# Second attention: the row maximum and the mask are written into PSUM by ScalarE, three matmul rounds follow, in a new order

## Chip, core and metric

The kernel runs on one core of one Trainium2 chip. The metric is the device time of one execution in microseconds (us). Most executions agree within 0.3%.

## What is computed

The network has four parts one after the other, each added to a residual `x` of 8 batches of 512 rows of 256 numbers (fp32): a first attention, a layer with 16 routed experts, a second attention and a layer with 8 routed experts. The change touches the second attention alone:

```
q = (layernorm(x) @ Wq) * 64 ** -0.5                    # 16 heads of 64
kv = concatenate([layernorm(ctx), layernorm(x)])        # 512 + 512 keys
k, v = kv @ Wk, kv @ Wv
sim = q @ k.T ; sim = sim - max(sim, over keys)
sim = where(mask, sim, -inf)                            # the mask concerns the first 512 keys
x = x + softmax(sim) @ v @ Wo
```

## The kernel before

`layer1_pairs` works in 64 steps: 8 batches times 8 pairs of heads. In step g the softmax and the output of pair g are computed while K, Q, the maxima (and in odd steps V for two pairs) of pair g + 1 are prepared. Head h of a pair lies on partitions 64h to 64h + 63, so two 64-row matmuls, one for each head, run at once; I call such two a round.

The units of a step, as the lists in `WHOLE` name them (one list for even steps, one for odd), and who works on each:

- KK and Q project K and Q of the next pair (L1796), three products each since every operand is split into a high and a low part (fp32r). ScalarE copies the high part (KH L1909, QH L1915), VectorE subtracts for the low part (KL L1956, QL L1961).
- VV0, VV1 project V (L1836, only in odd steps); ScalarE copies (L1921).
- S0 to S7 are rough scores with queries on the partitions (high parts only, L1848), for the row maximum; VectorE reduces them, S0 to S3 with the mask (L1976, two instructions for a tile), S4 to S7 without (L1981). N takes the minimum of the two halves' negated maxima (L1986).
- M brings the negated maxima from columns to rows: four matmuls against an identity (L1858); ScalarE copies into QM (L1925).
- ST0 to ST7 are the exact scores with keys on the partitions, 128 keys by 512 queries by two heads (L1871): four rounds, QM with KM (KM holds a row of ones and a row with the mask, brought by DMAs, L1735), QH with KL, QL with KH, QH with KH. ScalarE takes exp (L1936), GpSimd adds the eight exps up (L2032).
- PV0 to PV7 multiply by V into pO (fp32, L1805); O is ScalarE's copy of it (L1941). den sums the added exps over the keys of the previous step (fp32, L1882), ScalarE copies (L1929); r0 to r3 are reciprocals, after the last one VectorE also multiplies osb by them (L1992, L1996). YY is the product with Wo of the previous step (fp32, L1890), which VectorE adds to the residual (L2001).

Every engine goes through the same list of its parity in that order and does its own share of each unit, so the list is the order of every queue. Tiles of PSUM: pO and pm take one bank each, three slots of two banks serve the units named in `SLOTTED`, dealt in the order of the list, modulo 3 (`slot_of`). `slot_free` makes TensorE wait until the slot's last user has been read. M, Q and den share pm (`BANK`, `use`, `bank`). SyncE's list of DMAs loads weights every second step, K and V inputs once per batch, and the mask rows every step.

## Time and profile before

| | us |
|---|---|
| median of 3 runs | 3544.19 |
| lowest, highest | 3543.92, 3546.04 |
| profiled execution, its own time | 3545.06 |
| its span | 3543.5 |
| the second attention's steps, in the span | about 1054 to 2860 |

A row of the timeline has the start, the duration, the engine, the line, the operation with output and inputs, the count of merged instructions, and in brackets the idle time of the engine before it with what ended it. A matmul's duration is longer than the distance to the next, as they are pipelined.

### The profile page before, as it was taken

To read this page: it belongs to the slowest core of one execution; us is meant where nothing else is said; L and a number is where in the kernel's file an instruction comes from. 1 tells how busy PE (TensorE), PEld (TensorE's weight loads), DVE (VectorE), ACT (ScalarE), POOL (GpSimd) and SP (SyncE) were. 2 spreads that over 40 slices of the span, in tenths; PEclk is the share of its full clock that TensorE was granted. 3 is DMA by queue.
4 is the path that set the end of the run, shared out by engine and by line. 5 is a ranking of instruction groups with operands and counts; after the bars stand their busy time and mean duration, and the time that the engine had idled before them with its cause. 6 is when DMAs were issued, how large, how long until landed. Compare 5 with 4: busy or idle time off the path is not lost. (4 is left out here: it accounts for less than half of the span.)

```text
span 3543.5 us, 56159 instructions
## 1 busy us (share of the span) xinstructions
PE 3194.0 (90%) x17981; PEld 2294.0 (65%) x17982; DVE 2048.6 (58%) x4478; ACT 1267.7 (36%) x1778; POOL 1609.9 (45%) x929
## 2 busy tenths in 40 slices
PE   5875999999439999999999999999999966699988
PEld 4655888888425666666666666666666655577766
DVE  5656555555555666666766667666676653122235
ACT  2332333333234444444444444444444432122222
POOL 4002333333304665666656666556665635500037
PEclk7995999999769999999999999999999958899999
DMA  4000000000471010110101101011010031321223
GB/s 109 1 1 9 14 13 9 13 12 6 151 266 47 31 69 30 65 45 30 68 28 67 45 30 68 27 68 45 30 68 28 7 106 59 133 77 62 63 70 109
DMA packets 89978, 192.94 MB, mean 54 GB/s; under 512 B 12768, under 2 KB 58152, under 8 KB 83760
## 3 DMA queue, kind: packets, MB, share of 16 engines
q1 hardware_dynamic: 73856, 152.84, 12.5%
q0 software_dynamic: 11392, 27.36, 2.5%
q10 hardware_dynamic: 4656, 11.80, 1.0%
q8 instruction: 40, 0.66, 0.1%
q14 instruction: 34, 0.28, 0.0%
HBM read 137.60 MB, written 54.30 MB: 54 GB/s over the span
## 5 line engine op out<-in xcount | busy, mean ns | idle before, releaser
L2032 POOL TENSOR_TENSOR d_acc<-d_acc,d_pr 128x1024 f32<-128x1024 f32 x384 | 938.4, 2444 | 90.9 <-ACT d_pr L1936 60.5
L1936 ACT ACTIVATE d_pr<-d_p 128x1024 f32<-128x1024 f32 x512 | 487.4, 1026 | 235.8 <-PE d_p L1871 235.4
L1805 PE MATMUL d_pO<-d_pr,d_V 128*64 128x512 f32 x2048 | 473.0, 599 | 0.0
L2032 POOL TENSOR_TENSOR d_acc<-d_pr 128x1024 f32<-128x1024 f32 x64 | 153.5, 2399 | 619.8 <-ACT d_pr L1936 619.8
L1981 DVE TENSOR_REDUCE d_nm<-d_p 128x2 f32<-128x1024 f32 x256 | 304.5, 1221 | 95.1 <-PE d_p L1848 95.1
L1976 DVE CUSTOM_DVE_ANT_0 d_biased<-d_p,d_masked 128x512 f32<-128x512 f32 x512 | 330.6, 688 | 32.0 <-issue 32.0
L909 POOL TENSOR_TENSOR e_hs<-e_hf,e_hs 128x512 fp32r<-128x512 f32 x136 | 175.7, 1292 | 365.2 <-ACT e_hs L886 365.2
L1805 PEld LDWEIGHTS d_pO<-d_pr,d_V 128*64 128x64 f32 x2048 | 135.4, 136 | 261.4 <-issue 235.0
L939 DVE SCALAR_TENSOR_TENSOR res<-e_pY,m_Wt,res 128x256 f32<-128x256 f32 x544 | 225.7, 477 | 45.7 <-PE e_pY L847 44.9
L1992 DVE RECIPROCAL d_rb<-d_rb 128x128 f32<-128x128 f32 x256 | 224.6, 919 | 8.6 <-ACT d_rb L1929 8.6
L847 PEld LDWEIGHTS e_pY<-e_Wd,e_hs 128*128 128x128 f32 x1632 | 213.5, 191 | 13.7 <-POOL e_hs L909 2.2
L847 PE MATMUL e_pY<-e_Wd,e_hs 128*128 128x256 f32 x1632 | 217.2, 283 | 2.6 <-POOL e_hs L909 2.6
L930 DVE TENSOR_TENSOR e_hf<-e_sl,e_pU 128x512 f32<-128x512 f32 x136 | 93.7, 689 | 216.1 <-ACT e_sl L883 216.1
L831 PE MATMUL e_pG<-m_XH,e_Wgu 128*128 128x512 f32 x816 | 212.2, 395 | 4.2 <-issue 4.2
L1848 PE MATMUL d_p<-d_KH,d_QH 64*128 64x512 f32 x1024 | 208.4, 443 | 5.2 <-DVE d_nm L1976 2.5
L1848 PEld LDWEIGHTS d_p<-d_KH,d_QH 64*128 64x128 f32 x1024 | 89.0, 184 | 190.2 <-issue 127.9
L1871 PE MATMUL d_p<-d_QM,d_KM 64*128 64x512 f32 x1024 | 208.7, 402 | 0.0
L831 PE MATMUL e_pU<-m_XH,e_Wgu 128*128 128x512 f32 x816 | 208.3, 391 | 0.0
L1921 ACT COPY d_V<-d_p 128x1024 f32<-128x1024 f32 x64 | 64.8, 1012 | 400.2 <-PE d_p L1836 400.2
L1871 PE MATMUL d_p<-d_QH,d_KL 64*128 64x512 f32 x1024 | 202.3, 390 | 0.0
L1871 PE MATMUL d_p<-d_QL,d_KH 64*128 64x512 f32 x1024 | 201.8, 389 | 0.0
L1871 PE MATMUL d_p<-d_QH,d_KH 64*128 64x512 f32 x1024 | 201.7, 388 | 0.0
(288 smaller groups left out, 5621.8 us busy)
## 6 DMA issues: line engine op xcount, KB each, us to landing
d_W<-w_split SPq DMA_DIRECT2D x32, 1536.0 KB, 6.4
kv_split<-c_ys SPq DMA_DIRECT2D x16, 1024.0 KB, 6.4
d_kv<-kv_split SPq DMA_DIRECT2D x8, 2048.0 KB, 10.6
d_masked<-mask_bias SPq DMA_DIRECT2D x64, 256.0 KB
x_slots<-m_zeros SPq DMA_DIRECT2D x1, 9088.0 KB, 29.8
b_x<-x_slots SPq DMA_DIRECT2D x71, 128.0 KB, 2.0
y_slots<-b_y SPq DMA_DIRECT2D x71, 128.0 KB, 1.7
w_split<-c_wq POOLq DMA_DIRECT2D x4, 1536.0 KB, 8.3
```

Of the source, the lines that this page charges most:

```text
L831: last = pe.matmul(out[u % 2][0:fw, :], lhsT, XH[:, xp, k, n * S:(n + 1) * S], start=start, stop=(k == DC - 1 and (wp, xp) == PASSES[-1]))
L847: last = pe.matmul(pY[n % 2][:, t, :], hs[0:fw, u % 2, hp, t * P:(t + 1) * P], Wd[j][0:fw, wp, f, :], start=(f == 0 and m == 0 and t % 2 = ...
L909: pool.tensor_tensor(hs[0:fw, u % 2, LO, :], hf[0:fw, u % 2, :], hs[0:fw, u % 2, HI, :].bitcast(F32), ALU.subtract).then_inc(lo_done, 1)
L939: dve.scalar_tensor_tensor(res[:, tile, :], pY[n % 2][:, t, :], Wt[:, tile, bass.ds(e + column, 1)], res[:, tile, :], ALU.mult, ALU.add).t ...
L1805: last = pe.matmul(pO[own[h], :], V[vb][:, s, par * P + h * HD1:par * P + (h + 1) * HD1], pr[:, s % PT, h, :], start=(s == 0), stop=(s == ...
L1848: last = pe.matmul(out[:, h, :], QH[j][own[h], qt * P:(qt + 1) * P], KH[j][own[h], m * S:(m + 1) * S], start=True, stop=True)
L1871: last = pe.matmul(out[:, h, :], k_[own[h], s * P:(s + 1) * P], q_[own[h], :], start=(i == 0), stop=(i == len(terms) - 1))
L1936: act.activation(pr[:, n % PT, :, :], slot(st, what, n)[:, :, :], ACT.Exp).then_inc(exp_done, 1)
L1976: dve.tensor_tensor_reduce(biased[:, h, :], out[:, h, :], masked[j][:, :], -1.0, MASKED, ALU.add, ALU.min, nm2[:, j, h * TPB + qt, m:m + 1 ...
L1981: dve.tensor_reduce(both, out[:, :, :], AX.X, ALU.max, negate=True).then_inc(max_done, 1)
L1992: dve.reciprocal(rb[:, quarter], rb[:, quarter]).then_inc(r_done, 1)
L2032: pool.tensor_tensor(acc[:, q, :, :], a, pr[:, s % PT, :, :], ALU.add).then_inc(acc_done, 1)
```

## The change

In the transposed scores the round QM with KM goes. In its place the slot is filled before the matmuls: a new unit P0 to P7 on ScalarE writes, for the first four key tiles, the negated maximum plus the mask (`activation` Identity from `nmb`, with a bias column `mcol` for the mask), for the last four the negated maximum alone (`copy`). The three rounds left then accumulate upon it. M now makes the negated maximum in every partition for both heads: eight matmuls whose weights are a column of `nm` repeated (stride 0), into a slot instead of pm, and ScalarE copies 1024 columns to `nmb`. The slot of tile n is taken by P n; ScalarE waits until it is free. The mask comes as one column per key tile, by one DMA of 512 four-byte pieces; KM, its rows and the DMAs for them go. N writes eight numbers per partition side by side. The lists have a new order with P in it, and `start` is set once per bank in VV and YY.

```diff
 WHOLE = (
-    """M KK Q ST0 ST1 ST2 S0 S1 PV0 PV1 S2 ST3 S3 den PV2 PV3 S4 ST4 r0 ST5 r1 r2 ST6 ST7 S5 PV4 r3 PV5 PV6 PV7 O
-       S6 S7 YY N""".split(),
-    """Q KK M VV0 den S0 ST0 ST1 S1 ST2 ST3 ST4 ST5 ST6 r0 ST7 r1 r2 S2 r3 PV0 PV1 PV2 PV3 S3 S4 S5 PV4 PV5 PV6 PV7
-       S6 S7 VV1 N O YY""".split())
-BANK = ("M", "Q", "den")
+    """M Q P0 P1 KK ST0 ST1 S0 P2 den S1 ST2 S2 PV0 PV1 S3 P3 P4 ST3 ST4 S4 S5 P5 PV2 PV3 P6 PV4 P7 ST5 r0 r1 ST6 r2
+       ST7 r3 S6 PV5 PV6 PV7 S7 N O YY""".split(),
+    """Q M P0 VV0 ST0 P1 P2 KK ST1 ST2 den S0 P3 PV0 P4 PV1 ST3 r0 S1 ST4 PV2 S2 PV3 P5 P6 r1 ST5 S3 ST6 P7 PV4 PV5 r2
+       S4 ST7 S5 PV6 r3 PV7 S6 S7 VV1 N YY O""".split())
+BANK = ("Q", "den")
 SLOTS = 3
-SLOTTED = ("ST", "S", "KK", "VV", "YY")
+SLOTTED = ("P", "M", "S", "KK", "VV", "YY")
...
-        QM = sb("d_QM", [P, S], F32R)
+        nmb = sb("d_nmb", [P, 2, S])
+        mcol = [sb(f"d_mcol{j}", [P, TPB]) for j in range(2)]
...
-                            sp.wait_ge(st_done, NKT * st.g)
-                        for h in range(2):
-                            sp.dma_start(KM[j][h * HD1 + 1:h * HD1 + 2, :].bitcast(F32),
-                                         mb[bass.ds(bb, 1), :]).then_inc(mask_in[j], 16)
+                            sp.wait_ge(filled, NKT * st.g)
+                        sp.dma_start(mcol[j][:, :], mb[bass.ds(bb, 1), 0:S].rearrange("o (t p) -> p (o t)", p=P),
+                                     allow_slow_non_contiguous=True).then_inc(mask_in[j], 16)
...
-                            if k_ == "ST":
+                            if k_ == "P":
                                 pe.wait_ge(exp_done, NKT * s.g + m + 1)
+                            elif k_ == "M":
+                                pe.wait_ge(m_read, s.g + 1)
...
-            bank(what)
             pe.wait_ge(max_done, MAXES * st.g + MAXES)
-            for qt in range(TPB):
-                last = pe.matmul(pm[:, qt * P:(qt + 1) * P], nm[:, q, qt, :], identr[:, :], start=True,
-                                 stop=True)
-            last.then_inc(bank_done, 1)
+            out = slot_free(what)
+            for h in range(2):
+                for qt in range(TPB):
+                    last = pe.matmul(out[:, h, qt * P:(qt + 1) * P],
+                                     nm[:, q, h, qt:qt + 1].to_broadcast([P, P]), identr[:, :],
+                                     start=(qt == 0), stop=True, skip_group_check=True)
+            last.then_inc(m_done, 1)
...
                             if s == 0:
-                                pe.wait_ge(bank_read, use(st, "M"))
-                                pe.wait_ge(mask_in[q], 48 * st.by2 + 48)
                                 pe.wait_ge(k_lo, st.g + 1)
-                            out = slot_free(what, n)
-                            terms = [(KM[q], QM), (KL[q], QH[q]), (KH[q], QL[q]), (KH[q], QH[q])]
+                                pe.wait_ge(bank_read, use(step_before(st), "Q"))
+                            pe.wait_ge(filled, T + s + 1)
+                            out = slot(st, "P", n)
+                            terms = [(KL[q], QH[q]), (KH[q], QL[q]), (KH[q], QH[q])]
                             for i, (k_, q_) in enumerate(terms):
                                 for h in range(2):
                                     last = pe.matmul(out[:, h, :], k_[own[h], s * P:(s + 1) * P],
-                                                     q_[own[h], :], start=(i == 0), stop=(i == len(terms) - 1))
+                                                     q_[own[h], :], start=False, stop=(i == len(terms) - 1),
+                                                     skip_group_check=True)
...
-                            act.copy(QM[:, :], pm[:, :]).then_inc(bank_read, 1)
+                            act.wait_ge(m_done, st.g + 1)
+                            if not (isinstance(st.g, int) and st.g == 0):
+                                act.wait_ge(filled, NKT * st.g)
+                            act.copy(nmb[:, :, :], slot(st, what)[:, :, :]).then_inc(m_read, 1)
+                        elif what == "P":
+                            if n == 0:
+                                act.wait_ge(mask_in[q], 32 * st.by2 + 32)
+                                act.wait_ge(m_read, st.g + 1)
+                            for s, (k_, m) in slot_before(st, ("P", n)):
...
+                            if n < TPB:
+                                act.activation(slot(st, what, n)[:, :, :], nmb[:, :, :], ACT.Identity,
+                                               bias=mcol[q][:, n:n + 1]).then_inc(filled, 1)
+                            else:
+                                act.copy(slot(st, what, n)[:, :, :], nmb[:, :, :]).then_inc(filled, 1)
```

## Rows read from the trace of the kernel before

**Rows 1.** Page, section 2: busy tenths and granted clock (tenths) in 40 slices

```profile
PE   5875999999439999999999999999999966699988
...
PEclk7995999999769999999999999999999958899999
```

**Rows 2.** Steady loop: length; busy of PE, PEld, DVE, ACT, POOL; clock; DMA

```profile
1130.40:2795.00 1664.60, 1663.11 (x10212) 1065.24 (x10211) 1132.64 (x2222) 712.96 (x840) 1025.43 (x421) 1.00 0.13 46
```

**Rows 3.** Timeline of ScalarE, one pair of steps

```profile
2019.00 1.01 ACT L1921 COPY d_V<-d_p 128x1024 f32<-128x1024 f32 x1 [10.90 <-PE d_p L1836]
...
2026.51 2.86 ACT L1936 ACTIVATE d_pr<-d_p 128x1024 f32<-128x1024 f32 x3 [0.62 <-PE d_p L1871]
...
2074.44 1.01 ACT L1921 COPY d_V<-d_p 128x1024 f32<-128x1024 f32 x1 [10.88 <-PE d_p L1836]
```

**Rows 4.** Timeline of TensorE, even step

```profile
2020.92 2.98 PE L1796 MATMUL d_p<-d_kv,d_W 128*128 128x512 f32 x12
2023.74 1.52 PE L1796 MATMUL d_pm<-d_kv,d_W 128*128 128x512 f32 x6
2025.19 0.50 PE L1871 MATMUL d_p<-d_QM,d_KM 64*128 64x512 f32 x2
...
2025.99 0.40 PE L1871 MATMUL d_p<-d_QH,d_KH 64*128 64x512 f32 x2
...
2030.80 0.50 PE L1848 MATMUL d_p<-d_KH,d_QH 64*128 64x512 f32 x2
2031.13 0.39 PE L1871 MATMUL d_p<-d_QM,d_KM 64*128 64x512 f32 x2
```

**Rows 5.** Timeline of TensorE, odd step

```profile
2045.30 1.72 PE L1796 MATMUL d_pm<-d_kv,d_W 128*128 128x512 f32 x6
2046.86 2.89 PE L1796 MATMUL d_p<-d_kv,d_W 128*128 128x512 f32 x12
2049.59 0.56 PE L1858 MATMUL d_pm<-d_identr,d_nm 128*128 128x128 f32 x4
2049.99 3.08 PE L1836 MATMUL d_p<-d_W,d_kv 128*128 128x256 f32 x24
2053.00 1.08 PE L1882 MATMUL d_pm<-d_acc,d_ones 128*64 128x512 f32 x4
...
2062.54 3.65 PE L1805 MATMUL d_pO<-d_pr,d_V 128*64 128x512 f32 x16
2066.13 0.96 PE L1848 MATMUL d_p<-d_KH,d_QH 64*128 64x512 f32 x6
```

**Rows 6.** Timeline of TensorE's weight loads, even step

```profile
2028.50 0.19 PEld L1848 LDWEIGHTS d_p<-d_KH,d_QH 64*128 64x128 f32 x2 [0.48 <-ACT d_pr L1936]
```

**Rows 7.** Groups of ScalarE by form: busy, mean ns, idle before

```profile
L1915 ACT ACTIVATE d_QH<-d_pm 128x512 fp32r<-128x512 f32 x64 | 38.3, 599 | 128.1 <-PE d_pm L1796 128.1
...
L484 ACT ACTIVATE a_QT<-a_pQ,a_bqs 128x512 f32<-128x512 f32 x16 | 10.1, 684 | 18.8 <-PE a_pQ L318 18.8
...
L590 ACT COPY m_rows<-m_xh 128x1024 f32<-128x1024 f32 x4 | 4.2, 1040 | 2.0 <-PE m_px L614 2.0
```

**Rows 8.** Page, section 5: groups, busy and mean ns

```profile
L2032 POOL TENSOR_TENSOR d_acc<-d_acc,d_pr 128x1024 f32<-128x1024 f32 x384 | 938.4, 2444 | 90.9 <-ACT d_pr L1936 60.5
...
L1981 DVE TENSOR_REDUCE d_nm<-d_p 128x2 f32<-128x1024 f32 x256 | 304.5, 1221 | 95.1 <-PE d_p L1848 95.1
```

**Rows 9.** N: its line (min/median/max ns); timelines of VectorE and GpSimd

```profile
L1986 DVE TENSOR_TENSOR d_nm<-d_nm x64: 173/1359/1849, 1076.1 to 2823.1; 128x8 fp32r<-128x8 f32 x64
...
2018.09 1.82 DVE L1986 TENSOR_TENSOR d_nm<-d_nm 128x8 fp32r<-128x8 f32 x1
...
2004.66 15.23 POOL L2032 TENSOR_TENSOR d_acc<-d_acc,d_pr 128x1024 f32<-128x1024 f32 x6
```

**Rows 10.** Timeline of TensorE, end of the function

```profile
2827.50 0.63 PE L1871 MATMUL d_p<-d_QH,d_KL 64*128 64x512 f32 x2
2827.93 0.63 PE L1871 MATMUL d_p<-d_QL,d_KH 64*128 64x512 f32 x2
```

More of the change, by code:

```diff
@@ L1619, in use @@
     elif isinstance(st.g, int) and st.g == NSTEP:
-        before = 3 * NSTEP - 1
+        before = 2 * NSTEP - 1
     else:
-        before = 3 * st.g
+        before = 2 * st.g
     return before + bank_uses(st).index(kind) + 1
@@ L1689, in layer1_pairs @@
         MAXES = 3 * TPB + 1
-        SET_UP = 8
+        SET_UP = 2
         def maxes_before(n):
@@ L1713, in _ @@
                 sp.wait_ge(set_up, SET_UP)
-                for j in range(2):
-                    for h in range(2):
-                        sp.dma_start(KM[j][h * HD1:h * HD1 + 1, :].bitcast(F32), onerow[:, :].bitcast(F32)
-                                     ).then_inc(set_rows, 16)
-                sp.wait_ge(set_rows, 4 * 16)
                 sp.dma_start(W[1][:, :, :, :, :].bitcast(F32), wsp[1]).then_inc(w_in[1], 16)
@@ L1923, in emit @@
                         elif what == "M":
-                            act.wait_ge(bank_done, use(st, what))
-                            act.copy(QM[:, :], pm[:, :]).then_inc(bank_read, 1)
+                            act.wait_ge(m_done, st.g + 1)
[7 more added lines that the diff above has]
+                            for s, (k_, m) in slot_before(st, ("P", n)):
+                                if k_ == "P":
+                                    act.wait_ge(exp_done, NKT * s.g + m + 1)
+                                elif k_ == "M":
+                                    act.wait_ge(m_read, s.g + 1)
+                                elif k_ == "S":
+                                    act.wait_ge(max_done, MAXES * pair(s)[1] + maxes_before(m + 1))
+                                elif k_ == "KK":
+                                    act.wait_ge(k_lo, pair(s)[1] + 1)
+                                elif k_ == "VV":
+                                    act.wait_ge(v_read, values_before(s) + m + 1)
+                                else:
+                                    act.wait_ge(y_added, s.g + 1)
+                            if n < TPB:
+                                act.activation(slot(st, what, n)[:, :, :], nmb[:, :, :], ACT.Identity,
+                                               bias=mcol[q][:, n:n + 1]).then_inc(filled, 1)
+                            else:
+                                act.copy(slot(st, what, n)[:, :, :], nmb[:, :, :]).then_inc(filled, 1)
                         elif what == "den":
@@ L1935, in emit @@
                             act.wait_ge(acc_done, 7 * st.g + max(n, 1))
-                            act.activation(pr[:, n % PT, :, :], slot(st, what, n)[:, :, :], ACT.Exp
+                            act.activation(pr[:, n % PT, :, :], slot(st, "P", n)[:, :, :], ACT.Exp
                                            ).then_inc(exp_done, 1)
```

31 lines of the change are left out of this document (11 added, 20 removed).

## The prediction, made before the changed kernel was run

> **What bounds the kernel now.** I read the page first, to see which engine fills the span: in the slices that belong to this function (13 to 32) TensorE shows 9 tenths in every one, at full granted clock [rows 1]. The table by stretches says the same for the steady loop: in 1664.6 us TensorE is busy 1663.1, VectorE 1132.6, ScalarE 713.0, GpSimd 1025.4, the granted clock 1.00, which is the 2.4 GHz level [rows 2]. So the order written for TensorE is nearly free of waits, and what the change is worth is read from TensorE's issue times, not from busy shares (a matmul's bar overlaps the next one's).
>
> I then took the timeline of one pair of steps. The loop's two steps repeat: ScalarE's copy of V at 2019.00 [rows 3] has its twin at 2074.44, 55.44 us later. In the even step, projection of K takes 2.82 us and of Q 1.45; a round of two 64-row matmuls inside the transposed scores takes 0.23 (2025.19 to 2025.99 is 3 rounds and a 0.1 start) [rows 4]. In the odd step Q takes 1.56, M's four matmuls 0.40, VV0 3.01, den and what leads into the next unit 1.0, and four PV units 3.59 [rows 5]. A lone S between fp32 and fp32r work costs 0.33 [rows 4]; of the 3.59, the rounds themselves are 8 times 0.43, so one run of fp32 matmuls costs some 0.15 by itself and 0.10 on the S before it: 0.25 us per switch there and back. I call that the switch price.
>
> **What the change takes from TensorE.** Eight tiles per step lose one round of four: 16 rounds a pair at 0.23 make 3.7 us. M goes from 4 to 8 matmuls of the same shape: plus 0.4 a step, 0.8 a pair (if the stride-0 weights don't overlap with the matmuls, each could take twice 0.1 and M costs 1.6 more in a pair; if the copy is as cheap as now, nothing else; I take 0.1 each, as the row has the same 128x128 form). The new order has more runs of fp32 work: even step, den, PV0-1, PV2-4, PV5-7, YY, five where there were four; odd step seven (den, PV0-1, PV2, PV3, PV4-5, PV6-7, YY) where there were four. Four more at 0.25 are 1.0. The waits of today go: 0.48 before S1 in the even step [rows 6] and some 0.2 in the odd one, 0.7. Without any new wait the pair would be 55.4 - 3.7 + 0.8 + 1.0 - 0.7 = 52.8, 2.6 less. The loop has 31 full pairs: minus 80 us.
>
> **What it adds to ScalarE.** Eight fills of 128x1024 a step. No row shows ScalarE writing PSUM. The nearest is an SBUF to SBUF copy of that size, 1040 ns; a bias pointer costs 684 - 599 = 85 ns on 512 elements [rows 7], so the four masked fills are 1.11 and the four plain ones 1.02 to 1.04; following each other they overlap by 0.10 (three exps take 2.86 in all, one 1.02) [rows 3]. QM's copy of 512 becomes a copy of 1024: 0.59 to 1.01. That is 8.9 us a step on an engine that is busy 713.0 / 30 = 23.8 a pair, so 41.6 of 52.8. By its sum it fits. But a tile is now fill, matmuls, exp in one of three slots, and the slot is held for 1.0 + 0.7 + 1.0 plus two handoffs, where before the matmuls could take a slot that was just read. Bounds for a fill: 0.85 (a copy of 1024 takes 1.01 and one of 512 takes 0.60 [rows 3, 7], so 0.82 is left without the fixed part) to 1.2.
> The Trainium skill (ScalarE: Activation LUTs, Step-by-step: what each stage is for) says that ScalarE reaches PSUM with less latency than SBUF, with the caveat that this only helps if TensorE doesn't need most of PSUM. No row here shows such a write. By the first half the fills would lie at my lower bound, and the pair would be some 0.5 shorter; the caveat is what the next part prices.
>
> **The walk.** I followed one pair: each unit starts when its engine's previous one is done and its semaphores are there. From TensorE's last round to ScalarE's start it is 0.5 (2025.99 to 2026.51) [rows 3, 4]; from ScalarE or VectorE back to TensorE 0.15. S tiles leave VectorE 1.22 after their start [rows 8], the first four in two instructions that I take as long; a GpSimd addition takes 2.44 [rows 8]. Slots are dealt in the order of the list, modulo 3. Waits of TensorE that come out:
> (a) Even step, M at 0: ScalarE copies M to 2.2, QH 2.7 to 3.3, P0 to 4.3, P1 to 5.3, KH 5.5 to 6.5 (KK ends at 5.2), exp0 6.4 to 7.4. TensorE is through ST0 and ST1 at 6.6, and S0 takes P0's slot: it waits for exp0 until 7.55. 0.95.
> (b) P2 takes the slot of exp1 (to 8.4) and ends at 9.5; TensorE wants ST2 at 9.2. 0.45.
> (c) P3 waits for S1's maximum (10.7) and exp2, P4 for S2's, S4 for S3's, S5 for exp3. Small waits, 0.5 in all.
> (d) Odd step, after Q (1.55): M's slot 0 is the one that YY has just filled, as the even list now has 19 slotted units. So M waits until VectorE has added YY to the residual (1.22), and VectorE's list puts N in front of that. S7 is issued only behind PV7 and its maximum ends when YY ends. N takes 0.17 when free and 1.36 in the median, because it ends when a GpSimd addition ends: 2019.91, where GpSimd's chain ends at 2019.89 [rows 9]. With 1.4 for N the addition ends at 2.8, M goes at 2.95. 1.4. This N is hidden today (TensorE had YY and the next projection of Q between).
> (e) KK takes VV0's slot: ScalarE's copy of VV0 ends 1.2 after its last matmul, and only ST0 (0.7) stands between. 0.65.
> (f) Odd step further on, each behind a fill that itself waits for an exp in the same slot: ST3 0.2, ST5 0.3, ST7, PV7 and S0 0.1 each. 0.8.
> Sum 4.75, for which the walk's own total, with switches that fall into a wait not paid twice, is 57.4 against 55.4: plus 2.0 a pair.
> On (d), the Trainium skill (SBUF — State Buffer, Who interferes with whom) states that a VectorE operation with two SBUF inputs and a GpSimd one that reads SBUF exclude each other for a whole instruction. By the row of N alone its cost ends at 1.85; by the rule it could be a whole addition, 2.44, and the pair 1.0 longer than in my sum.
>
> **What is nothing.** The removed rows of KM (three DMAs a step become two, one of them of 512 four-byte pieces) are issued a step ahead of use on a queue that is idle most of the time; W's and kv's loads behind them have 20 us of cover; if that cover were gone it would cost the transfer once per step, 2 us or more. Head of the function: four small DMAs and memsets less in front of the second weight load, under the first load anyway, 0 to -3. Last step: GpSimd's seven additions set it, and they start one fill and copy later, +2. Exp, copy and identity alternate already without a table load in the loop, so none is added.
>
> **Rivals.**
> 1. The saving stays: PSUM holds TensorE up only at (a) and (e), which don't hang on a fill's length, and the rest is hidden by a lead TensorE carries or by quicker fills and a free port for N. Then 52.8 + 1.6 = 54.4, minus 1.0 a pair: 3544 - 31 = 3513; with half of the others back, some 3537. For it: TensorE's total is truly less, and (b), (c), (f) are waits of 0.1 to 0.45 each, as small as my error on one. Against: three slots, every tile now passes ScalarE twice, and (a), (d), (e) are long. Chance 0.24 for faster, 0.07 for within 0.2%.
> 2. The forecast, slot waits outweigh the saving: 31 x 2.0 = 62. Chance 0.50 for 3580 to 3640, 0.09 for less than that but slower (3551 to 3580), if N mostly finds the port free: (d) falls to 0.3 and the pair is +0.9, 3573. This one decides as soon as waits exceed 2.6 a pair.
> 3. The clock goes too. Where TensorE was held up, at the end of the function, its granted level fell to 1.2 GHz and a round took 0.43 (2827.50 to 2827.93) in place of 0.23 [rows 10]; the clock line is under 9 tenths only in slices where the busy line is too [rows 1]. If a twentieth of the loop ran at that level, the pair would be 2.5 longer still: 3606 + 78 = 3684. With it I count fills or M at their upper bounds, 3650 and more. Chance 0.10.
> The Trainium skill (TensorE: Matmul & The Clock Gate, A second HAM failure mode: psum-queue depth-cycling) says that short, frequent idling between groups of matmuls can make the clock swing. Waits of at most 1.4 us in 57, as forecast, come nearer to the loop of today (clock 1.00) than to the end of the function, so I keep it small.
>
> **How the numbers follow.** The profiled execution took 3545.1, its span 3543.5, the median of the runs 3544.2: the sum holds for the median too. Likeliest 3544.2 + 62 = 3606. The range goes down to 3512, the point where only (a) and (e) hold, and up to 3660. A measurement of this kernel tells 0.2% from no change, 7 us. Faster 0.24, same 0.07, slower 0.69.
>
> **What would show it.** In the profile after: a pair of steps takes 57 us (V's copies); TensorE shows waits of about 1 us before S0 of the even step and before M of the odd one, 0.6 before KK there; idle time before the scores' matmuls is put down to ScalarE's fills and exps; ScalarE is busy 73% of the loop; N lies in front of the residual's addition and ends with a GpSimd addition. A fill lasts 1.02 or 1.11. Wrong I am if the pair is below 55.4: then (d) is hidden, or the fill is far shorter than a copy. If the clock in the loop is below 1.00, rival 3 holds.

## The result, and the profile after

The changed kernel takes 3648.8 us in the median of four runs (3636.8 to 3663.2) against 3544.1 for the kernel before, run beside it: a ratio of 1.030, interval 1.0276 to 1.0321. It is slower, on the side that was forecast and inside the range, but by 105 us where 62 were forecast, and just above the stretch that was held likeliest (3580 to 3640). Its profiled execution has a span of 3638.8 us, 95.3 above before's 3543.5.

The page of the changed kernel, section 2, has the two lines that answer to [rows 1]:

```profile
PE   5876999999249999999999999999999975789988
...
PEclk8995999999669999999999999999999967999999
```

TensorE still fills the function's slices. The table by stretches says it more closely; this one is cut at the ends of ScalarE's V copies, so that it holds exactly 30 pairs of steps (columns as in [rows 2]):

```profile
1135.63:2889.30 1753.67, 1692.56 (x9481) 989.54 (x9480) 1128.30 (x2220) 1222.89 (x1320) 1020.31 (x420) 0.99 0.13 44
```

1753.67 / 30 is 58.46 us a pair, against 55.45 before (the same copies stand at 1131.71 and 2795.18 there). 30 times 3.01 is 90 of the 95 us of span; the other 5 lie outside. TensorE's idle time has gone from 1.5 us [rows 2] to 61.1, and the granted clock shows 0.99. ScalarE is busy 1222.9, 70% of the loop (forecast 73%). So the question is what three microseconds a pair are made of.

The mean hides three kinds of pairs. Here are three copies of V in ScalarE's timeline of the changed kernel, as in [rows 3]:

```profile
2011.70 1.01 ACT L1921 COPY d_V<-d_p 128x1024 f32<-128x1024 f32 x1 [4.91 <-PE d_p L1832]
2048.02 1.01 ACT L1921 COPY d_V<-d_p 128x1024 f32<-128x1024 f32 x1 [2.18 <-PE d_p L1832]
2072.23 1.01 ACT L1921 COPY d_V<-d_p 128x1024 f32<-128x1024 f32 x1 [4.91 <-PE d_p L1832]
```

This pair lasts 60.53. Of the 30, 14 last 56.3 to 57.0, 7 last 58.8 to 59.1, and 9 last 60.3 to 61.9. What sets the long ones apart is seen at the end of the even step (timeline of all engines, the changed kernel; POOL adds the softmax's row sums, L2019 is the output's transpose OT, L2005 two row maxima, L2009 is N, L2024 the residual addition):

```profile
2033.40 7.59 POOL L2048 TENSOR_TENSOR d_acc<-d_acc,d_pr 128x1024 f32<-128x1024 f32 x3 [0.46 <-ACT d_pr L1960]
...
2033.89 2.44 DVE L2019 TENSOR_TENSOR d_OT<-d_osb,d_rb 128x512 f32<-128x512 f32 x1
...
2036.25 2.34 DVE L2005 TENSOR_REDUCE d_nm<-d_p 128x2 f32<-128x1024 f32 x2
...
2038.63 2.39 DVE L2009 TENSOR_TENSOR d_nm<-d_nm 128x8 fp32r<-128x8 f32 x1
...
2040.94 1.21 DVE L2024 TENSOR_TENSOR res<-res,d_p 128x1024 f32 x1
```

N, eight elements a partition, takes 2.39 us and ends at 2041.02, where GpSimd's third addition ends at 2040.99. Behind it comes the residual's addition, and for that M of the odd step waits, because its slot holds YY. TensorE's timeline of the same stretch, which answers to [rows 5]:

```profile
2036.88 1.99 PE L1889 MATMUL d_p<-d_Wo,d_OT 128*128 x8
...
2038.52 1.74 PE L1792 MATMUL d_pm<-d_kv,d_W 128*128 128x512 f32 x6
...
2042.39 1.10 PE L1855 MATMUL d_p<-d_identr,d_nm 128*128 128x128 f32 x8 [2.14 <-DVE res L2024]
...
2043.34 4.57 PE L1832 MATMUL d_p<-d_W,d_kv 128*128 128x256 f32 x24
...
2049.08 3.01 PE L1792 MATMUL d_p<-d_kv,d_W 128*128 128x512 f32 x12 [0.28 <-ACT d_V L1921]
```

TensorE stands idle 2.14 before M, and then the 24 multiplications of VV0 take 4.57 in place of the 3.08 of [rows 5]: the engine has been granted less. The table by stretches has it, in the third column from the end (1.00 is the 2.4 GHz level, 0.50 the 1.2 GHz level): full when M starts, half within VV0, full again before VV0 ends.

```profile
2042.00:2043.00 1.00, 0.61 (x5) 0.61 (x6) 0.75 (x2) 0.00 (x0) 0.00 (x0) 1.00 0.00 0
2044.00:2045.00 1.00, 1.00 (x6) 1.00 (x6) 0.00 (x0) 0.82 (x2) 0.00 (x0) 0.50 0.00 0
2047.00:2048.00 1.00, 1.00 (x10) 0.87 (x10) 0.00 (x0) 0.00 (x0) 0.00 (x0) 1.00 0.00 0
```

In the 14 short pairs N takes 0.17, the idle time before M is 0.13 at most and VV0 takes 3.09. In the 7 middle ones N takes 2.39 and VV0 3.09; in the 9 long ones both are long. N's line in the changed kernel shows the two kinds (min, median and max in ns), and the twin of that timeline from a short pair shows how little divides them:

```profile
L2009 DVE TENSOR_TENSOR d_nm<-d_nm x64: 166/168/2397, 1075.4 to 2915.9; 128x8 fp32r<-128x8 f32 x64
```

```profile
2213.30 7.64 POOL L2048 TENSOR_TENSOR d_acc<-d_acc,d_pr 128x1024 f32<-128x1024 f32 x3 [0.47 <-ACT d_pr L1960]
...
2218.52 0.17 DVE L2009 TENSOR_TENSOR d_nm<-d_nm 128x8 fp32r<-128x8 f32 x1
```

The single records of the 30 even steps show this: in 28 of them N's start and that of GpSimd's third addition lie within 0.01 us of each other. It is a tie. Where the addition wins (16 times), N waits for the whole of it; where N wins, the addition ends some 0.05 later. In the last two N is 0.06 ahead. And the tie is no accident. In the step above, GpSimd's first addition ends at 2035.78; OT, which takes 0.69 by itself (x1 below), has waited for that and ends at 2036.33. From 2035.78 on VectorE has 0.55 of OT and 2.34 of maxima to do, and GpSimd an addition of 2.68 (2035.86 to 2038.54): both are ready for the next at 2038.6. The kernel's own runs differ by 26 us, those of x1 and x9 below, where the tie costs nothing, by 4. That would fit a tie that falls differently from run to run, but only one run of the changed kernel has a trace.

The even step, which answers to [rows 4], shows the wait forecast as (a), TensorE idle 0.60 before S0:

```profile
2018.36 0.50 PE L1869 MATMUL d_p<-d_QH,d_KL 64*128 64x512 f32 x2
...
2019.62 0.40 PE L1869 MATMUL d_p<-d_QH,d_KH 64*128 64x512 f32 x2
...
2020.62 0.49 PE L1845 MATMUL d_p<-d_KH,d_QH 64*128 64x512 f32 x2 [0.60 <-ACT d_pr L1960]
```

The fills are what they were taken for; section 5 of the page (columns: busy time, mean ns, idle before):

```profile
L1946 ACT ACTIVATE d_p<-d_nmb,d_mcol 128x1024 f32<-128x1024 f32 x256 | 281.9, 1121 | 6.2 <-ACT d_nmb L1927 4.8
...
L1949 ACT COPY d_p<-d_nmb 128x1024 f32<-128x1024 f32 x256 | 253.9, 1016 | 2.1
```

Last, TensorE's groups over the 30 pairs: columns are busy time, mean ns, idle before. The kernel before, window 1131.71 to 2795.18:

```profile
L1805 PE MATMUL d_pO<-d_pr,d_V 128*64 128x512 f32 x1920 | 443.5, 598 | 0.0
L1871 PE MATMUL d_p<-d_QM,d_KM 64*128 64x512 f32 x960 | 194.9, 401 | 0.0
L1848 PE MATMUL d_p<-d_KH,d_QH 64*128 64x512 f32 x960 | 194.1, 441 | 1.5
L1871 PE MATMUL d_p<-d_QH,d_KL 64*128 64x512 f32 x960 | 189.3, 389 | 0.0
...
L1836 PE MATMUL d_p<-d_W,d_kv 128*128 128x256 f32 x1440 | 186.7, 286 | 0.0
...
L1858 PE MATMUL d_pm<-d_identr,d_nm 128*128 128x128 f32 x240 | 39.1, 285 | 0.0
```

The changed kernel, window 1135.63 to 2889.30:

```profile
L1801 PE MATMUL d_pO<-d_pr,d_V 128*64 128x512 f32 x1920 | 470.1, 606 | 0.0
L1869 PE MATMUL d_p<-d_QH,d_KL 64*128 64x512 f32 x960 | 216.9, 448 | 1.2
L1845 PE MATMUL d_p<-d_KH,d_QH 64*128 64x512 f32 x960 | 213.0, 459 | 17.9 <-ACT d_pr L1960 17.9
L1832 PE MATMUL d_p<-d_W,d_kv 128*128 128x256 f32 x1440 | 201.1, 300 | 0.0
...
L1792 PE MATMUL d_p<-d_kv,d_W 128*128 128x512 f32 x720 | 178.4, 396 | 8.3 <-ACT d_V L1921 8.3
...
L1855 PE MATMUL d_p<-d_identr,d_nm 128*128 128x128 f32 x480 | 69.2, 287 | 33.7 <-issue 18.0 <-DVE res L2024 15.0
```

The last row puts more than half of the idle time before M down to "issue". In the single records M starts 0.10 or 0.24 after the residual's addition ends, in all 30 pairs, so that addition is what ended the wait in each.

Bars of neighbouring groups overlap, so these sums can't be subtracted as they stand. I took the single multiplications of the same windows and counted each from the end of the one before it, or from its own start if that is later; I call this its occupied time. This gives a ledger without double counting (us a pair, occupied time of TensorE unless "idle"; the last two columns belong to experiments below):

| | before | changed | changed, no collision (x1) | changed, no fills, no collision (x7) |
|---|---|---|---|---|
| round QM x KM | 4.03 | - | - | - |
| round QH x KL, now the first of a tile | 3.69 | 5.42 | 5.42 | 4.90 |
| the other two rounds | 7.35 | 7.42 | 7.42 | 7.40 |
| S | 5.29 | 5.79 | 5.79 | 5.81 |
| PV | 14.33 | 15.11 | 15.11 | 15.11 |
| M | 0.79 | 1.95 | 1.92 | 1.92 |
| VV | 5.99 | 6.47 | 5.98 | 5.98 |
| Q and KK | 8.27 | 8.59 | 8.59 | 8.57 |
| den, YY | 5.68 | 5.68 | 5.68 | 5.68 |
| idle before S | 0.05 | 0.60 | 0.60 | 0.69 |
| idle before M | 0 | 1.12 | 0.05 | 0.05 |
| other idle | 0 | 0.32 | 0.32 | 0.28 |
| pair | 55.45 | 58.46 | 56.88 | 56.38 |

### The profile page after: what moved, and what is told of

Same layout as the page of the kernel before. It is cut to its first block and busy times, and to the rows that moved or that the text cites. A ratio compares the mean times of both kernels' runs of the same rounds, so it can differ in the third digit from the quotient of the medians.

```text
span 3638.8 us, 55024 instructions
## 1 busy us (share of the span) xinstructions
PE 3221.1 (89%) x17213; PEld 2210.9 (61%) x17214; DVE 2043.8 (56%) x4478; ACT 1811.7 (50%) x2290; POOL 1602.5 (44%) x923
## 5 line engine op out<-in xcount | busy, mean ns | idle before, releaser
L1960 ACT ACTIVATE d_pr<-d_p 128x1024 f32<-128x1024 f32 x512 | 501.2, 1025 | 112.5 <-PE d_p L1869 112.3
L1801 PE MATMUL d_pO<-d_pr,d_V 128*64 128x512 f32 x2048 | 503.7, 609 | 0.1
L2005 DVE TENSOR_REDUCE d_nm<-d_p 128x2 f32<-128x1024 f32 x256 | 300.9, 1216 | 45.0 <-PE d_p L1845 45.0
L1946 ACT ACTIVATE d_p<-d_nmb,d_mcol 128x1024 f32<-128x1024 f32 x256 | 281.9, 1121 | 6.2 <-ACT d_nmb L1927 4.8
L1980 DVE TENSOR_TENSOR d_KL<-d_p,d_KH 128x1024 fp32r<-128x1024 f32 x64 | 78.4, 1225 | 357.8 <-ACT d_KH L1909 357.8
L1801 PEld LDWEIGHTS d_pO<-d_pr,d_V 128*64 128x64 f32 x2048 | 121.8, 136 | 235.2 <-issue 161.5
L1949 ACT COPY d_p<-d_nmb 128x1024 f32<-128x1024 f32 x256 | 253.9, 1016 | 2.1
L1845 PE MATMUL d_p<-d_KH,d_QH 64*128 64x512 f32 x1024 | 228.1, 461 | 23.7 <-ACT d_pr L1960 20.3
L1869 PE MATMUL d_p<-d_QH,d_KL 64*128 64x512 f32 x1024 | 232.6, 450 | 7.7 <-ACT d_p L1946 5.8
L883 ACT ACTIVATE e_sl<-e_pG 128x512 f32<-128x512 f32 x136 | 81.3, 598 | 280.3 <-PE e_pU L831 280.3
L1832 PE MATMUL d_p<-d_W,d_kv 128*128 128x256 f32 x1536 | 213.2, 299 | 0.0
```

The lines of the kernel that those rows point to most:

```text
L1801: last = pe.matmul(pO[own[h], :], V[vb][:, s, par * P + h * HD1:par * P + (h + 1) * HD1], pr[:, s % PT, h, :], start=(s == 0), stop=(s == ...
L1845: last = pe.matmul(out[:, h, :], QH[j][own[h], qt * P:(qt + 1) * P], KH[j][own[h], m * S:(m + 1) * S], start=True, stop=True)
L1869: last = pe.matmul(out[:, h, :], k_[own[h], s * P:(s + 1) * P], q_[own[h], :], start=False, stop=(i == len(terms) - 1), skip_group_check=True)
L1946: act.activation(slot(st, what, n)[:, :, :], nmb[:, :, :], ACT.Identity, bias=mcol[q][:, n:n + 1]).then_inc(filled, 1)
L1949: act.copy(slot(st, what, n)[:, :, :], nmb[:, :, :]).then_inc(filled, 1)
L1960: act.activation(pr[:, n % PT, :, :], slot(st, "P", n)[:, :, :], ACT.Exp).then_inc(exp_done, 1)
```

## The experiments

The theory after seeing the trace: the pair pays 1.6 us for the collision of N with GpSimd (1.05 of waiting, 0.5 of lower clock), and the rest, 1.4 us, is what the three-round tile and its new order cost more than they save. Rivals: the fills on ScalarE as the main cost; the new order as the main cost; a collision that the kernel before pays as well.

**x1: the collision taken away by small sums.** The changed kernel, GpSimd adding 16 columns instead of 1024; the rest of the softmax's row sums is left out.

```diff
...
-                        pool.tensor_tensor(acc[:, q, :, :], a, pr[:, s % PT, :, :], ALU.add).then_inc(acc_done, 1)
+                        pool.tensor_tensor(acc[:, q, :, 0:8], a, pr[:, s % PT, :, 0:8], ALU.add).then_inc(acc_done, 1)
```

> The changed kernel, GpSimd's additions of the exps cut from 1024 columns to 16 (2 times 8; the denominators are wrong, so this part of the result is left out). In the changed kernel a pair of steps takes 56.9 us in 13 of 30 pairs, where N lasts 0.17, and 58.9 to 61.9 in 17, where N lasts 2.39; in 9 of these the VV0 behind it takes 4.6 in place of 3.1. Theory: N collides with a GpSimd addition, the residual's addition and M wait behind it, and the clock falls only after that wait. Then every pair is at 56.3 to 57.0, VV0 at 3.1, clock 1.00, and the time 3640 - 31 x 1.6 = 3590. Rival 1, the clock falls from the many short waits, whatever N does: VV0 still at 4.6 in a third of the pairs, time 3605 to 3615. Rival 2, N is slow for another reason: nothing changes, 3640 to 3650.

3592.6 us, ratio 1.0135 (1.0118 to 1.0152). N takes 0.17 in every pair, OT 0.69, VV0 3.08, every full pair is a short one (mean 56.88), the clock 1.00. As the theory had it: collision and clock together are 56 of the 105 us. (Of the 30 pairs of the table above 14 are short and 16 long, one more and one fewer than the text put down beforehand has it.)

**x2: the same cut in the kernel before.**

> The kernel before, GpSimd's additions of the exps cut from 1024 columns to 16 (the denominators are wrong: that part of the result is left out), as in the run of the changed kernel with small sums. Theory: N's wait for the shared port is hidden in the kernel before, since the residual's addition comes ahead of it and K or Q are projected before M needs N: pair 55.4, time 3544 within 0.2%. Rival, the collision costs as much there, up to 1.4 a pair: 3500 to 3530, and then it isn't the change that exposed it.

3536.2 us, 0.9976 (0.9967 to 0.9986). N falls from a median of 1.36 us [rows 9] to this:

```profile
L1986 DVE TENSOR_TENSOR d_nm<-d_nm x64: 166/172/175, 1075.8 to 2821.9; 128x8 fp32r<-128x8 f32 x64
```

The pair stays at 55.44. In the trace of the kernel before N takes 1.0 us in one step of each pair and 1.8 in the other, in all 60 steps of the loop; so that kernel has the collision in every step and pays nothing for it. Between the last S and M its lists give TensorE YY, K and Q to do, or VV1 and YY. Of the 8 us that are gone 7 lie at the function's end, where GpSimd's additions set the last step; I had not allowed for that.

**x3: N behind YY.** The changed kernel with two entries of the even list exchanged, so that VectorE adds the residual first and N comes after it.

```diff
-       ST7 r3 S6 PV5 PV6 PV7 S7 N O YY""".split(),
+       ST7 r3 S6 PV5 PV6 PV7 S7 YY N O""".split(),
```

> The changed kernel, in the even list N moved behind YY (S7 YY N O), so VectorE adds YY to the residual first and N after. Theory: the residual's addition is no longer behind the collision, N asks 1.2 later and ends with the same GpSimd addition, so M waits 1 to 1.3 less in the bad pairs and some 0.7 more in the good ones: every pair 57.2 to 57.8, and if the wait is then short enough the clock doesn't fall: time 3600 to 3622. If it falls still, 3625 to 3640. Rival, M's wait isn't set by N and the residual's addition: no change, 3640 to 3650.

3620.8 us, 1.0213 (1.0196 to 1.023); 27 of the 30 pairs take 57.7 to 57.8, the last three less. VectorE and TensorE in one pair (two views of the timeline):

```profile
2029.92 1.22 DVE L2024 TENSOR_TENSOR res<-res,d_p 128x1024 f32 x1 [0.32 <-PE d_p L1889]
2031.06 0.98 DVE L2009 TENSOR_TENSOR d_nm<-d_nm 128x8 fp32r<-128x8 f32 x1
```

```profile
2032.18 1.10 PE L1855 MATMUL d_p<-d_identr,d_nm 128*128 128x128 f32 x8 [0.91 <-DVE d_nm L2009]
```

N now comes in the middle of an addition and pays what is left of it, 0.98. M waits 0.91, and the clock does not fall: VV0 takes 3.09 at most in all 30 pairs. An exchange of two list entries takes 28 us off.

**x9: N with one operand.** The tie itself removed: the same minimum as one reduction over the innermost axis.

```diff
-                            halves = nm2[:, j, :, :].rearrange("p (o t) m -> p o t m", o=2)
-                            dve.tensor_tensor(nm[:, j, :, :], halves[:, :, :, 0], halves[:, :, :, 1], ALU.min
-                                              ).then_inc(max_done, 1)
+                            dve.tensor_reduce(nm[:, j, :, :].rearrange("p o t -> p (o t)"), nm2[:, j, :, :], AX.X, ALU.min
+                                              ).then_inc(max_done, 1)
```

> The changed kernel, in which VectorE's last minimum of a step (N) is made as one reduction over the innermost axis of its operand, so that it reads one operand from SBUF instead of two halves of it. Nothing is left out; GpSimd's additions are whole. Theory of the collision (VectorE with two operands in SBUF waits for a whole addition of GpSimd, with one it does not): N takes about 0.2 us in every pair, the even step's matrix M is never late, VV0 takes 3.1 us and the clock stays up; the output's transpose (two operands) still takes 2.4 us in the even step, at no cost; every pair 56.9 us, 3593 to 3602 us in all, ratio 1.014 to 1.0165. Rival (VectorE waits for GpSimd whatever it reads): N 2.4 us in more than half of the pairs, mean pair about 58.5, 3640 to 3655 us.

3592.1 us, 1.0136 (1.0119 to 1.0153), with GpSimd's sums whole. N's line and the 30 pairs:

```profile
L2008 DVE TENSOR_REDUCE d_nm<-d_nm x64: 169/170/171, 1077.4 to 2869.7; 128x8 fp32r<-128x16 f32 x64
```

```profile
1137.61:2843.14 1705.53, 1676.62 (x9481) 973.24 (x9480) 1095.62 (x2219) 1223.39 (x1320) 1020.57 (x420) 1.00 0.14 45
```

56.85 a pair. OT, with two operands, still takes some 2.4 in each even step and costs nothing. So it is not "GpSimd is busy" but "two operands from SBUF while GpSimd adds". (The new N is also another instruction, a reduction; this run cannot part the two.) This is the best form of the changed kernel that I found, and it is still 48 us slower than the kernel before.

**x4: the round saved, nothing else.** The kernel before without the round QM x KM; the row maximum and mask are left out of the scores.

```diff
-                            terms = [(KM[q], QM), (KL[q], QH[q]), (KH[q], QL[q]), (KH[q], QH[q])]
+                            terms = [(KL[q], QH[q]), (KH[q], QL[q]), (KH[q], QH[q])]
```

> The kernel before with the round of QM and KM left out and nothing in its place (maximum and mask are left out of the exps), old order. Rival 1, TensorE alone counts: 16 rounds of 0.23 a pair, 55.4 - 3.7 = 51.7, time 3427. Theory: with shorter tiles TensorE runs into the slots, which are emptied by ScalarE's exps at about 1 us each: half of the saving comes back as waits, pair 53.5, time 3480 to 3490.

3494.4 us, 0.9859 (0.9843 to 0.9875), pair 53.83. Of 4.03 us that the round occupied, 1.6 came off the pair. TensorE's groups over a stretch as long as its 30 pairs (1131 to 2746) show where the rest went:

```profile
L1871 PE MATMUL d_p<-d_QH,d_KL 64*128 64x512 f32 x960 | 204.4, 422 | 1.4
L1848 PE MATMUL d_p<-d_KH,d_QH 64*128 64x512 f32 x960 | 203.6, 461 | 22.0 <-ACT d_pr L1936 12.2 <-DVE d_nm L1976 9.7
```

In the ledger: 0.93 to the tile's new first round (0.34 of it the start of a tile, which the round that is gone had carried), 0.54 to S, and 0.79 of idle time. The idle time is ended by exps and by maxima, which empty slots: the three slots could just keep four rounds fed; three rounds they can't. So the most that the change could win in the old order, with the maximum and mask for nothing, is 50 us.

**x6 and x7: no fills.** The changed kernel without the P's (maximum and mask left out; the first round starts the sum), x6 with whole sums, x7 with small ones.

```diff
-                            pe.wait_ge(filled, T + s + 1)
-                            out = slot(st, "P", n)
+                            out = slot_free("P", n)
...
-                                                     q_[own[h], :], start=False, stop=(i == len(terms) - 1),
+                                                     q_[own[h], :], start=(i == 0), stop=(i == len(terms) - 1),
```

> The changed kernel without the eight fills (negative maximum and mask left out), full sums. Theory: N's collision with GpSimd is still there, so the pair is bimodal as before, its good value 56.1 to 56.4 and its bad one 58 to 60: time 3600 to 3640. Rival, without fills TensorE has so much room that N is hidden: 3480 to 3540.

3647.7 us (3638.6 to 3670.3), 1.030 (1.0256 to 1.0344): sixteen fills of a microsecond fewer in each pair and no gain in the time. The tie is there as before and falls worse: N takes 2.40 in 24 of 30 pairs where it was 16, VV0 up to 5.4. The mean pair is 59.0, the good ones 56.1 to 56.5. So x6 by itself says nothing of the price of the fills.

> The changed kernel with small sums (pair 56.88, no collision) and without the eight fills: each tile takes its slot itself and its first round overwrites (negative maximum, mask and full denominators are left out), same lists, same slots, three rounds. Theory: the long waits (a) before S0 and (e) before KK don't hang on fills and stay; (b) before ST2 and those in front of ST3 to ST7 go: pair 56.1 to 56.4, so the fills cost at most 0.8 of the 4.1 that the pair is over 52.8. Rival, ScalarE's extra work is the whole cost: the pair falls to 53 to 54.

3566.4 us, 1.0063 (1.0046 to 1.0079), pair 56.38. Against x1 that is the price of the fills with all else equal: 0.50 a pair, and the ledger has it at one place, the first round (5.42 against 4.90). The other two rounds, which add to what ScalarE wrote, take 7.42 with fills and 7.40 without. The times differ by more, 26 us: 15 are the 30 pairs, 9 lie behind them, in the function's last step, and 2 in front.

```profile
L1868 PE MATMUL d_p<-d_QH,d_KL 64*128 64x512 f32 x960 | 208.5, 430 | 0.0
```

What x7 has over x4 (56.38 against 53.83), with the same three rounds and no fills in either, is the new order with the wider M: PV 0.78, M 1.13, the first round 0.28, Q and KK 0.28, idle 0.2 (S and YY are 0.1 less).

**x12: the new order in the kernel before.** Four rounds, M in its old place with four multiplications; small sums.

```diff
-    """M KK Q ST0 ST1 ST2 S0 S1 PV0 PV1 S2 ST3 S3 den PV2 PV3 S4 ST4 r0 ST5 r1 r2 ST6 ST7 S5 PV4 r3 PV5 PV6 PV7 O
-       S6 S7 YY N""".split(),
-    """Q KK M VV0 den S0 ST0 ST1 S1 ST2 ST3 ST4 ST5 ST6 r0 ST7 r1 r2 S2 r3 PV0 PV1 PV2 PV3 S3 S4 S5 PV4 PV5 PV6 PV7
-       S6 S7 VV1 N O YY""".split())
+    """M Q KK ST0 ST1 S0 den S1 ST2 S2 PV0 PV1 S3 ST3 ST4 S4 S5 PV2 PV3 PV4 ST5 r0 r1 ST6 r2 ST7 r3 S6 PV5 PV6 PV7 S7
+       N O YY""".split(),
+    """Q M VV0 ST0 KK ST1 ST2 den S0 PV0 PV1 ST3 r0 S1 ST4 PV2 S2 PV3 r1 ST5 S3 ST6 PV4 PV5 r2 S4 ST7 S5 PV6 r3 PV7
+       S6 S7 VV1 N YY O""".split())
```

> The kernel before with one part of the change: the order of work of the changed kernel (its two lists without the P's). The row maximum and the mask still go through the fourth round, M still takes four multiplications. GpSimd's sums are cut to 16 columns, as in the other kernels with small sums (left out: the rest of the softmax's row sums), so that no collision with VectorE comes in; it is to be read against the kernel before with small sums (55.44 us a pair, 3536 us) and the changed kernel without fills and with small sums (56.38 us a pair). Theory (the new order by itself costs 1.0 to 1.8 us a pair: three more runs of PV at 0.26 us each by TensorE's occupied time in the two traces, more runs of S and ST, and waits at their borders): a pair at 56.4 to 57.2 us, 3565 to 3590 us. Rival (the order costs nothing; what the changed kernel loses beside the collision is M's eight multiplications and the slots held from the fill on): a pair at 55.3 to 55.7 us, 3530 to 3545 us.

3720.7 us, 1.0495 (1.0478 to 1.0513), pair 61.33: neither theory. The order needs M out of the bank that it shares with Q. TensorE's timeline:

```profile
2025.18 1.72 PE L1796 MATMUL d_pm<-d_kv,d_W 128*128 128x512 f32 x6
2028.47 0.66 PE L1858 MATMUL d_pm<-d_identr,d_nm 128*128 128x128 f32 x4 [1.57 <-DVE d_QL L1961]
2028.96 3.08 PE L1836 MATMUL d_p<-d_W,d_kv 128*128 128x256 f32 x24
...
2060.51 1.67 PE L1796 MATMUL d_pm<-d_kv,d_W 128*128 128x512 f32 x6 [0.68 <-ACT d_QM L1925]
```

M waits until VectorE has read Q from the bank, and Q until ScalarE has read M. Those two waits (1.56 and 0.67 a pair in the mean) and VV's 0.49 by the clock make 2.7 of the 5.9 us. What the order's borders cost is in its ledger beside x2's: PV 15.11 against 14.33, the first round 4.88 against 4.02, S 5.63 against 5.28, 2.0 us a pair in all, with no fill and no collision anywhere. (The last 1.2 are Q, K and M behind their waits, 0.7, and idle time before S, 0.4.) PV has 8 runs a pair instead of 5 (0.26 for each new one), the transposed scores 11 instead of 5. So the run does not show the price of the order in the changed kernel, where M is out of the bank, but it gives the borders' price a second time: the same 0.78 for PV.

**x10: the old order in the changed kernel.** The old lists, with the P's put in as early as the slots allow.

```diff
+    """M P0 KK P1 Q ST0 P2 ST1 ST2 S0 S1 P3 PV0 PV1 S2 ST3 S3 den PV2 PV3 S4 P4 P5 ST4 P6 r0 P7 ST5 r1 r2 ST6 ST7 S5
+       PV4 r3 PV5 PV6 PV7 O S6 S7 YY N""".split(),
+    """Q KK M VV0 P0 P1 den S0 ST0 ST1 S1 P2 P3 P4 ST2 ST3 P5 ST4 P6 P7 ST5 ST6 r0 ST7 r1 r2 S2 r3 PV0 PV1 PV2 PV3 S3
+       S4 S5 PV4 PV5 PV6 PV7 S6 S7 VV1 N O YY""".split())
```

> The changed kernel with the order of work of the kernel before: its two lists, with each P (a fill) set as far ahead of its tile's ST as that list's free slots allow. Nothing is left out. Theory (the third slot that each tile now holds from its fill on, and ScalarE's eight fills, make the old order dearer than the new one; the new order is a repair of that and no cause of the loss): runs of two or three ST in the old lists wait for fills, a pair comes to 62 to 66 us, 3750 to 3880 us in all. Rival (the new order is itself what loses, and the fills fit in the old order as well): a pair at 56 to 58 us, 3570 to 3640 us, not slower than the changed kernel.

3943.8 us, 1.1125 (1.1105 to 1.1144), pair 68.3 where at most 66 was expected. The table of waits has, for the matmuls of the scores (total us, times, longest):

```profile
PE d_p L1869 <- ACT d_p L1946: 92.3, 75, 1.6
PE d_p L1869 <- ACT d_p L1949: 82.7, 75, 1.8
```

TensorE stands idle 175 us for fills between 1130 and 2840, 7.0 a pair, against 0.04 a pair in the changed kernel. The granted clock of the 30 pairs is 0.94 where the changed kernel has 0.99, so part of the 68.3 is the clock. A run of six ST in the old odd list asks for a tile each 0.7 us, and ScalarE has a fill and an exponential to do for each, 2.1. So, with the fills placed as they are here, the new order is a repair: it spreads the ST's, and pays for that in borders.

**x5 and x8: other orders.** The changed kernel with lists found by a hand walk, x5 for the shortest pair, x8 with N's collision hidden.

> The changed kernel with other lists (same units, same work; VV0 ahead of Q and KK in the odd step, fills further ahead of their tiles, den and PVs between S0 and the tiles whose slots it waits for). Theory: the waits belong to order and slots, so a walk along these lists gives 56.0 a pair without N's collision, time about 3561. Rival, ScalarE's writes into PSUM themselves, or the adding upon them, slow TensorE: the pair stays at 56.9 or over, 3590 to 3650.

> The changed kernel, same work, full sums, lists that keep N and the residual's addition away from M whatever N lasts (N early in the even step with YY, PV6 and PV7 behind it, VV0 between M and Q in the odd step, den and PV0 between a tile and the S that takes its slot). Theory: the loss is the order's, and with N covered the pair is 55.5 to 56.3 at clock 1.00, time 3550 to 3575. Rival, the fills and the three slots cost in any order: 56.9 or more, 3590 to 3650.

3689.5 us (1.0404, 1.0387 to 1.0421) and 3713.8 us (1.0479, 1.0461 to 1.0496): both misses, by 128 us and by 139 or more. In x5, whose forecast left the collision out, N takes 2.35 once in nearly every pair and VV0 about 4.6 in most; without both the pair would still be about 57.5, not 56.0. In x8 N is free, and the collision sits in OT, for which YY now waits:

```profile
2009.57 2.75 DVE L2019 TENSOR_TENSOR d_OT<-d_osb,d_rb 128x512 f32<-128x512 f32 x1
...
2012.47 3.33 PE L1889 MATMUL d_p<-d_Wo,d_OT 128*128 x8 [2.09 <-DVE d_OT L2019]
```

YY's eight multiplications take 3.33 behind that wait, and 1.99 above without one. A walk that knows neither the collisions nor the clock is off by more than the differences that it is asked to find.

**x11: half of it.** Tiles 0 to 3 with four rounds, 4 to 7 with a fill and three; N with one operand; lists of its own.

```diff
+                            if n in FILLED:
+                                pe.wait_ge(filled, len(FILLED) * st.g + FILLED.index(n) + 1)
+                                out = slot(st, *tile(n))
+                            else:
+                                pe.wait_ge(m_read, st.g + 1)
+                                out = slot_free("ST", n)
+                                for h in range(2):
+                                    pe.matmul(out[:, h, :], KM[own[h], :], nmb[own[h], h, :], start=True, stop=False,
+                                              skip_group_check=True)
```

> A mixture: tiles 0 to 3 of each function are made as in the kernel before (four rounds, the first of a constant with the row maximum, the mask as the exponential's bias), tiles 4 to 7, which need no mask, as in the changed kernel (ScalarE's copy, three rounds); lists made for it by a hand walk; N as one reduction over one operand. Nothing is left out. Theory (a round saved is worth 0.23 us of TensorE and gives back some 0.44 us of its 16 a pair only as long as ScalarE has room; half of the fills fall away, so do half of the slots' waits): a pair of 55.2 to 55.8 us, 3545 to 3568 us, ratio 1.000 to 1.007. Rival (the loss is the order with fills at all, not their number): a pair above 56.5 us, 3590 us or more. If every saved round were kept: 8 rounds x 0.23 = 1.85 us a pair off, 3490 us.

3619.6 us, 1.021 (1.0193 to 1.0227), pair 57.99: the rival's number. 1.36 of it are idle time, most of it here (view of waits):

```profile
PE d_p L1906 <- DVE d_nm L2028: 33.2, 30, 1.4
```

That is YY behind a maximum of VectorE, in each pair 1.1 us, which my walk did not have. And TensorE's occupied time is 56.64, above before's 55.40: eight rounds saved are 1.64 (2.39 for the constant's eight rounds against 4.03), but PV gives back 0.76, M 0.89, the round QH x KL 0.58, and Q and K 0.45. The borders and the wider M are paid in full for half of the saving.

## Why the prediction was right or wrong

The sign, the range and the kind of cause (waits and borders outweigh the saving, ScalarE's sum fits) were right; 43 of the 105 us were missing. By the terms:

- **The round, 3.7.** The term itself is right (4.03 occupied, 0.35 of it the start of a tile, which only moves to the next round). Wrong was to take it as a gain with 0.7 on top for old waits. x4 shows what is left of it in the old order: 1.6. The waits of [rows 6] that I credited stand in the weight loads' timeline, where TensorE itself lost 0.05 a pair, and with a round gone new ones open in front of S. This step failed by 0.7 for the credit. The 2.4 that x4 doesn't keep are mostly waits for slots; my sum has waits of that kind only in (a) to (f), and had put some of them down to fills.
- **M, 0.8.** 1.16 measured. A weight load with stride 0 was not the reason as far as the row shows: the eight multiplications take 287 ns each as the four took 285, and follow each other at 0.11 as those did. Eight more of them are 0.9; the other 0.24 is the first one behind Q's projection, 0.30 where it was 0.06.
- **Borders, 1.0.** PV 0.78, Q and KK 0.32, 1.1 in all: the switch price of 0.25 holds (0.26 for each run of PV in two kernels). What the tiles' own borders cost was not in my sum. The single records of x7 and x12, which have no fills, show it: a tile's first round occupies 0.23 behind another tile or an S and 0.43 behind PV, V, K or Q. In the kernel before 1 tile of 16 stands behind such work, in the new order 6 do: five more at 0.2.
- **(a) 0.95:** idle 0.60 and 0.17 of start, from the last round's end (2019.62 and 0.23) to 2020.62: 0.77.
- **(b), (c), (f), 1.75 together:** the ledger's first round grew by 1.73, of which 0.34 is the moved start; the fills' part of it is 0.50 to 0.52 by x1 against x7. The rest, 0.87, is the tiles' borders of the new order, not the fills behind which I had put it; x12, with no fill, has 0.86.
- **(e) 0.65:** 0.44 in the odd step above (the last round of ST0 starts at 2048.41 and so ends at 2048.64; KK starts at 2049.08).
- **(d) 1.4.** The place, the chain (YY's slot, the residual's addition, N in front of it, M behind) and the cause were named, and the mean came out near: M's idle time is 1.12 over 30 pairs. That is luck, for the term was read wrongly. 1.36 is the median of [rows 9] between steps at 1.0 and steps at 1.8; in the loop no N took it. There N arrives in the middle of an addition; in the changed kernel it arrives at an addition's start: 0.17 in 14 pairs, 2.39 in 16, nothing between, and M's idle time is about 2 where N waits and 0.13 at most elsewhere. What hides N at that place in the kernel before is YY and the projections of Q and K; the new order still has YY and Q there and moves K's behind M. The Trainium skill (SBUF — State Buffer, Who interferes with whom) has the rule of the whole instruction, which I had quoted and not used; the trace agrees with it, for N at 2.39 and OT at 2.44, and x9 agrees with its other half, that one SBUF operand is free. The pair did come out 1.0 longer than in my sum, as I had said for that case, but not by this wait.
- **The clock, rival 3.** Taken as a case of its own at one in ten; it came on top of the forecast. VV0 at 4.56 to 5.42 in 9 of 30 pairs is 0.48 a pair in the ledger, 14 us in the loop. I had set it aside with "waits of at most 1.4". Where it fell the wait was 2.0 to 2.2, so (d), near in the mean, failed here by the size of the single wait.
- **ScalarE's fills** were right: 1121 and 1016 ns against 1.11 and 1.02 to 1.04.

Where the missing 43 us are: with N free the prediction had +0.9 a pair and 3573; measured without the collision it is +1.4 and 3592 (x1, x9), so the steady terms were some 20 us short. The credit of 0.7, M's 0.3 and the tiles' borders of 0.9 are more than that; the errors partly cancelled, since the fills took 0.5 where (b), (c) and (f) had 1.75. The collision was priced at 1.1 a pair on top and took 1.58, 56 us of the time: its waits 1.07, as forecast, and the clock 0.48. So each half of the miss has its own cause, and neither is the fills.

The change of the pair, 3.01, in steps of one trace to the next: the round gone, -1.62 (x4); the new order with the wide M, +2.55 (x7); the fills, +0.50 (x1); the collision with the clock, +1.58.

Not settled: what the order costs in the changed kernel taken alone, since x12 adds the shared bank to it, and no run has the wide M in the old order without fills; and why a wait of about 2 us was followed by the lower clock in 9 pairs and not in 7.

## What to carry to other kernels

A saving on the engine that bounds is only kept as far as its suppliers have room: take the work away without any replacement first (x4), and see what is left, before paying for a replacement; here 1.6 of 4.0 us were, and the borders of the order that the replacement needed cost more than that. Give a small VectorE operation that others wait for a single SBUF operand whenever GpSimd works beside it; it costs nothing and here it was worth 56 us. And price a lock by both its outcomes, free and a whole instruction of the other engine, not by the median seen in another schedule.

## What the runs showed of the hardware

- **A lock that forms its own tie.** N needs 0.17 us, and took that or 2.39 as it started within 0.01 us of an addition of GpSimd. An earlier collision (OT, 2.44) had let VectorE go at an addition's end and so set it in step with GpSimd; 2.9 us of work on VectorE and one addition of 2.68 on GpSimd with the gap before the next then brought both to the same instant. Where it falls otherwise, N takes what is left of the addition, 0.98 in x3.
- **The clock after a single wait in a full loop.** TensorE had been at full granted clock; behind idle times of 2.0 to 2.2 us before M, VV0 took 3.09 in 7 pairs and 4.56 to 5.42 in 9. Behind 0.91 (x3) it never did; in x12, behind 1.57, it did in 10 of 30 pairs, and YY took 3.33 instead of 1.99 behind 2.09 (x8). The granted clock is back at 1.00 before VV0 ends (2047 in the table above).
- **ScalarE writing PSUM.** A copy of 128x1024 from SBUF to PSUM took 1016 ns, from PSUM to SBUF 1.01 us (V's copy), from SBUF to SBUF 1040 [rows 7]. The column of the mask as a bias adds 105 ns. The Trainium skill (ScalarE: Activation LUTs, Step-by-step: what each stage is for) says that PSUM is nearer to ScalarE; here the direction is worth some 20 ns in 1040. The fills came at 1.02 and 1.12, not at the 0.85 of my lower bound, so the shorter pair that hung on it did not come.
